# Conv-attention-MoE hybrid: q product in natural order, two softmax shifts on TensorE, the apply by quarters

## The reference

```python
q = einsum('bchw,oc->bohw', x, wq) + bq     # 16 channels
k = einsum('bchw,oc->bohw', x, wk) + bk     # 16 channels
v = einsum('bchw,oc->bohw', x, wv) + bv     # 128 channels
energy = einsum('bci,bcj->bij', qf, kf).reshape(b, h, w, h, w)
attn = softmax(energy, axis=-1)             # over the last 16
out = einsum('bchk,bhwkv->bcwv', v, attn)
x = gamma * out + x
```

## Time and profile before

| | us |
|---|---|
| median of 3 runs | 186.25 (186.21 to 189.31) |
| the profiled execution, its own time | 186.13 |
| its span, first to last instruction | 184.2 |
| outside the span | 1.9 |

### The profile page before, as it was taken

One profiled execution on the slowest core, in us unless ns is written; L12 is line 12 of the kernel. 1 busy time (PEld: TensorE's weight loads), 2 busy tenths in 40 slices (PEclk: granted clock), 3 DMA queues, 4 the chain that ended last, 5 costly groups with the idle time before them and its releaser, 6 DMA issues.

```text
span 184.2 us, 3336 instructions
## 1 busy us (share of the span) xinstructions
PE 174.1 (95%) x1277; PEld 118.6 (64%) x1277; DVE 117.1 (64%) x199; ACT 123.2 (67%) x185; POOL 79.5 (43%) x68
## 2 busy tenths in 40 slices
PE   6999999989898998999999999999999999999991
PEld 3267867665466544447466567567887888888880
DVE  1569544985465396456084959397888677676673
ACT  3516953317727743545988598867878999999970
POOL 8404228988703284452536093524151152333312
PEclk9999999999999999999999999999999999999999
DMA  5799200000000000570000000000000880000001
GB/s 141 276 374 419 96 0 0 4 0 4 0 5 0 2 0 4 181 271 7 0 0 5 0 0 0 4 0 0 0 7 4 244 269 0 0 4 0 0 0 57
DMA packets 5791, 10.94 MB, mean 59 GB/s; under 512 B 1280, under 2 KB 1664, under 8 KB 5520
## 3 DMA queue, kind: packets, MB, share of 16 engines
q1 hardware_dynamic: 5360, 10.65, 16.7%
q10 hardware_dynamic: 416, 0.08, 0.3%
HBM read 10.17 MB, written 0.56 MB: 58 GB/s over the span
## 4 chain that ended last, share of the span: by engine, by line
PE 73%; issue 8%; ACT 7%; POOL 4%; DVE 4%; DMA 2%; ACTq 0%; DVEq 0%; POOLq 0%
PE PS L1159 9%; PE PS L1163 7%; PE PS L1160 7%; PE PS L1186 6%; PE PS L1189 6%; PE PS L1187 6%; PE PS L1181 4%; POOL pairs L357 4%; PE PS L1017 3%; PE PS L1031 3%; ACT room L516 2%; PE PS L910 2%; PE PS L878 2%; PE PS L1104 2%; DMA convw_sb<-convw 2%
## 5 line engine op out<-in xcount | busy, mean ns | idle before, releaser
L516 ACT ACTIVATE room<-PS,b_sb 128x512 f32<-128x512 f32 x64 | 43.6, 688 | 22.6 <-PE PS L1163 21.2
L772 DVE TENSOR_TENSOR Gl<-room,Gh 128x512 fp32r<-128x512 f32 x50 | 41.2, 831 | 13.7 <-ACT Gh L461 13.0
L365 POOL TENSOR_TENSOR x_sb<-x_sb,room 128x512 f32<-128x512 f32 x15 | 23.6, 1572 | 56.0 <-DVE room L781 56.0
L1159 PE MATMUL PS<-x2h,w1h 128*128 128x512 f32 x64 | 27.4, 427 | 1.2 <-ACT room L516 0.8
L461 ACT ACTIVATE Gh<-room 128x512 fp32r<-128x512 f32 x40 | 25.3, 633 | 1.3
L1163 PE MATMUL PS<-x2l,w1h 128*128 128x512 f32 x64 | 25.5, 398 | 0.0
L1160 PE MATMUL PS<-x2h,w1l 128*128 128x512 f32 x64 | 25.2, 393 | 0.0
L1186 PE MATMUL PS<-Gh,w2h 128*128 128x512 f32 x50 | 20.8, 416 | 0.0
L1187 PE MATMUL PS<-Gh,w2l 128*128 128x512 f32 x50 | 19.8, 395 | 0.0
L1189 PE MATMUL PS<-Gl,w2h 128*128 128x512 f32 x50 | 19.7, 395 | 0.0
L1159 PEld LDWEIGHTS PS<-x2h,w1h 128*128 128x128 f32 x64 | 12.0, 187 | 10.6 <-issue 4.9
(11 more groups left out here) (136 smaller groups left out, 294.2 us busy)
## 6 DMA issues: line engine op xcount, KB each, us to landing
room<-comb_rows SPq DMA_DIRECT2D x16, 256.0 KB, 5.2
w1raw<-w SPq DMA_DIRECT2D x8, 256.0 KB, 5.9
w_sb<-w SPq DMA_DIRECT2D x2, 1024.0 KB, 10.6
x_sb<-x SPq DMA_DIRECT2D x2, 256.0 KB, 3.2
dev<-xk SPq DMA_DIRECT2D x1, 512.0 KB, 6.3
out<-x_sb SPq DMA_DIRECT2D x2, 256.0 KB, 4.2
attw_sb<-attw SPq DMA_DIRECT2D x1, 320.0 KB, 6.8
cst<-consts SPq DMA_DIRECT2D x1, 228.5 KB, 6.5
```

The lines of the kernel that those rows point to most:

```text
L365: nc.gpsimd.tensor_tensor(t2[:, cols(p)], t2[:, cols(p)], part[:, s, :], ALU.add).then_inc(acc_done, 1)
L516: nc.scalar.activation(G[:, n % GR, :], PS[:, U_BANK[n % 2], :], ACT.Gelu, bias=b1_sb[:, c:c + 1])\
L772: nc.vector.tensor_tensor(Gl[:, n % GR, :], G[:, n % GR, :], Gh[:, n % GR, :].bitcast(f32), ALU.subtract)\
L1159: mm(o, w1h[e][:, ms], x2h[:, cols(p)], start=True, stop=False)
```

## The change

- q is computed with x in its natural order; the copies by ScalarE and VectorE now read PSUM with h innermost, a stride of 16 elements (`by_columns`), and write `cq` as before.
- `shift(q)` for q = 2 and 3 only takes the negated maximum; TensorE adds it to bank q by a product of the identity with the maxima, each repeated 16 times (`subtract_max`), and ScalarE's exp reads PSUM. VectorE's order becomes shift 0, 1, 2, sums 0, shift 3, sums 1, 2, 3, scale 3.
- The constants' load has a semaphore of its own (`ident_in`).
- `conv_values` goes by halves of two blocks, with its own place in the order; the turns stand between them.
- `conv_apply` goes by quarters: 4 calls of 32 products each, with 64 moving columns in place of 128. All four stand behind the last values.

```diff
-            sp.dma_start(cst[:, :], consts).then_inc(cst_in, 16)
+            sp.dma_start(cst[:, :], consts).then_inc(ident_in, 16)
...
-                nc.scalar.activation(cq[0:C8, pair, :, :, 0].rearrange("c b w h -> c (b w h)"), PS[64:64 + C8, p, :],
+                nc.scalar.activation(cq[0:C8, pair, :, :, 0], by_columns(PS[64:64 + C8, p, :]),
...
             def conv_exp(q):
-                act.wait_ge(shifted, q + 1)
-                nc.scalar.activation(A[:, q * W4:(q + 1) * W4, :, :], S[:, q], ACT.Exp).then_inc(exp_ready, 1)
+                if q < DVE_SHIFTS:
+                    act.wait_ge(shifted, q + 1)
+                    src = S[:, q]
+                else:
+                    act.wait_ge(lowered, q - DVE_SHIFTS + 1)
+                    src = PS[:, q, :].rearrange("p (w k v) -> p w k v", w=W4, k=K8)
+                nc.scalar.activation(A[:, q * W4:(q + 1) * W4, :, :], src, ACT.Exp).then_inc(exp_ready, 1)
...
-                nc.vector.tensor_scalar(cq[32:32 + C8, pair, :, :, 1].rearrange("c b w h -> c (b w h)"),
-                                        PS[64:64 + C8, p, :], convb_sb[64:64 + C8, 0:1], None, ALU.add)\
+                nc.vector.tensor_scalar(cq[32:32 + C8, pair, :, :, 1], by_columns(PS[64:64 + C8, p, :]), convb_sb[64:64 + C8, 0:1], None, ALU.add)\
...
             def shift(q):
-                nc.vector.tensor_reduce(cmax[:, q], e, AX.X, ALU.max).then_inc(cmax_ready, 1)
+                nc.vector.tensor_reduce(cmax[:, q], e, AX.X, ALU.max, negate=(q >= DVE_SHIFTS)).then_inc(cmax_ready, 1)
+                if q >= DVE_SHIFTS:
+                    return
...
-            shift(0)
-            shift(1)
+            for q in range(3):
+                shift(q)
             sums(0)
-            shift(2)
+            shift(3)
             sums(1)
-            shift(3)
             sums(2)
             sums(3)
             scale(3)
...
-                mm(PS[64:64 + C8, p, :].rearrange("c (b w h) -> c b w h", b=2, w=W),
-                   convw_sb[:, 0:C8], x_sb[:, cols(p)].rearrange("c (b h w) -> c b w h", b=2, h=H),
-                   start=True, stop=True)
+                mm(PS[64:64 + C8, p, :], convw_sb[:, 0:C8], x_sb[:, cols(p)], start=True, stop=True)
...
+            def subtract_max(q):
+                pe.wait_ge(ident_in, 16)
+                pe.wait_ge(cmax_ready, q + 1)
+                mm(PS[:, q, :].rearrange("p (g v) -> p g v", v=W), ident,
+                   cmax[:, q].unsqueeze(2).broadcast_to([128, W4 * K8, W]),
+                   start=False, stop=True, skip_group_check=True).then_inc(lowered, 1)
...
-            def conv_apply(g):
-                if g == 0:
+            def conv_apply(q):
+                if q == 0:
                     pe.wait_ge(vT_ready, 2)
-                pe.wait_ge(A_ready, 2 + g)
-                if g:
+                if q < WQ - 1:
+                    pe.wait_ge(A_ready, q + 1)
+                else:
                     pe.wait_ge(last_A_ready, 1)
                 for k in range(K8):
                     for b in range(B):
                         rows = slice(32 * b, 32 * (b + 1))
-                        last = mm(PS[:, 4 + b, g * 128:(g + 1) * 128], vT[rows, k, :],
-                                  A[rows, 8 * g:8 * (g + 1), k, :], start=(k == 0), stop=(k == K8 - 1))
+                        last = mm(PS[:, 4 + b, q * 64:(q + 1) * 64], vT[rows, k, :],
+                                  A[rows, W4 * q:W4 * (q + 1), k, :], start=(k == 0), stop=(k == K8 - 1))
...
-            for q in range(WQ):
-                energy(q)
-                turn(1)
-            for i in range(2):
-                conv_values(i)
-            turn(2)
-            conv_apply(0)
-            turn(1, 0)
-            conv_apply(1)
-            pe.wait_ge(cst_in, 64)
+            energy(0)
+            turn(1)
+            energy(1)
+            conv_values(0, 0)
+            energy(2)
+            energy(3)
+            subtract_max(2)
+            conv_values(0, 1)
+            turn(1)
+            subtract_max(3)
+            conv_values(1, 0)
+            turn(1)
+            conv_values(1, 1)
+            turn(1)
+            for q in range(WQ):
+                conv_apply(q)
+            pe.wait_ge(cst_in, 48)
```

More of the change, by code:

```diff
@@ L151, in hybrid_program @@
         convw_in, attw_in, cst_in = sem("convw_in"), sem("attw_in"), sem("cst_in")
+        ident_in, lowered = sem("ident_in"), sem("lowered")
         w1_in, w2_in = [sem(f"w1_in{e}") for e in range(E)], [sem(f"w2_in{s}") for s in range(2)]
@@ L192, in cols, with by_columns @@
             return slice(p * HALF, (p + 1) * HALF)
+        def by_columns(images):
+            return images.rearrange("c (b h w) -> c b w h", b=2, h=H)
         RAW_BANKS = [((4, 5), (6, 7)), ((2, 3), (4, 5)), ((6, 7), (2, 3)), ((4, 5), (6, 7))]
@@ L219, in hybrid_program @@
         WARM_BANK = [3, 4, 0, 1]
+        DVE_SHIFTS = 2
         U_BANK, Y_BANK, GATE_BANK = (0, 1), (2, 3), (3, 4)
@@ L539, in _ @@
             norm_dev(2)
-            act.wait_ge(cst_in, 64)
+            act.wait_ge(ident_in, 16)
+            act.wait_ge(cst_in, 48)
             for n in range(2):
@@ L622, in _ @@
             scale(3)
-            dve.wait_ge(cst_in, 64)
+            dve.wait_ge(ident_in, 16)
+            dve.wait_ge(cst_in, 48)
             dve.wait_ge(gamma_in, 16)
@@ L879, in energy, with conv_values @@
                                   cq[:, b, W4 * q + w, :, :].rearrange("c h k -> c (h k)"), ck[:, b, :],
-                                  start=True, stop=True)
+                                  start=(w == 0), stop=(q < DVE_SHIFTS and w == W4 - 1), skip_group_check=True)
                 last.then_inc(energy_done, 1)
-            def conv_values(i):
-                if i == 0:
+            def subtract_max(q):
[4 more added lines that the diff above has]
+                   start=False, stop=True, skip_group_check=True).then_inc(lowered, 1)
+            def conv_values(i, half):
+                if i == 0 and half == 0:
                     pe.wait_ge(xk_in_s, 16)
-                for k in range(4 * i, 4 * i + 4):
+                for k in range(4 * i + 2 * half, 4 * i + 2 * half + 2):
                     last = mm(PS[:, 4 + i, (k % 4) * C:(k % 4 + 1) * C], x_k[:, k, :], convw_sb[:, QK:QK + C],
                               start=False, stop=True, skip_group_check=True)
-                    if k % 4 == 1:
-                        turn(1)
-                last.then_inc(vT_done, 1)
+                if half:
+                    last.then_inc(vT_done, 1)
             def conv_bias(i):
@@ L909, in conv_apply @@
                         rows = slice(32 * b, 32 * (b + 1))
-                        last = mm(PS[:, 4 + b, g * 128:(g + 1) * 128], vT[rows, k, :],
-                                  A[rows, 8 * g:8 * (g + 1), k, :], start=(k == 0), stop=(k == K8 - 1))
-                        if g and k == K8 - 1:
+                        last = mm(PS[:, 4 + b, q * 64:(q + 1) * 64], vT[rows, k, :],
+                                  A[rows, W4 * q:W4 * (q + 1), k, :], start=(k == 0), stop=(k == K8 - 1))
+                        if q == WQ - 1 and k == K8 - 1:
                             last.then_inc(conv_done, 1)
```

## The result

The changed kernel takes 189.38 us (median of 5 runs, 189.09 to 190.21) against 186.25: the ratio is 1.0171, interval 1.014 to 1.0201, so it is slower by some 3.1 us. (Runs in a slower state of the chip, such as the 189.31 of before, are left out of all ratios.) The prediction said 188.8, 2.7 slower.

What follows compares the result with a forecast made beforehand. TensorE, busy 95% of the span, was taken as the bound. Apply start 18.25 plus 7.35 plus 0.15 drain gave 25.75 against 23.05, so 186.13 + 2.7 = 188.8 us; range 187.0 to 190.3.

Steps and rivals of the forecast that it cites:

- The mark and the pass-through: End of conv's apply on TensorE, 23.05 before: whatever moves it moves the run; forecast 25.75, +2.7 us, no slack behind.
- Part 4: Apply by quarters: 256 records in place of 128, each still costing its weight load, 28.8 ns; 7.35 us plus 0.15 drain.
- Rival A: Apply: half the columns cost half the time, loads hidden by the stream; -0.75, 185.4 us; chance 0.09.
- Part 1: q projection on TensorE: contiguous records 0.43 against 0.86, ending 1.7 us earlier; waiting for bv cuts the gain to 0.75.
- Part 2: Two subtractions moved from VectorE, 0.61 each there, to TensorE: four records of 0.43, 1.72 us in all.
- rival C: Subtractions on TensorE: the repeated operand streams at half rate, 1.7 us more, 190.5 us; chance 0.05.
- rival B: Copies of q: strided PSUM reads cost double, energy(0) starts at 9.75 after all; +0.75, 189.5 us; chance 0.10.
- From energy(0) to the apply: TensorE's energies, subtractions, turns and values, then ScalarE's copy: energy(0) at 9.0, apply(0) at 18.25, against 18.50 before.
- Part 3: VectorE's saved 1.2 us is lost because exp 3 follows the values' copy on ScalarE; scaling done at about 21.1, before 20.91.
- Rival D: TensorE idles from 6.3 to 7.25, so the clock drops to 1.2 GHz; 4 us lose 2, 190.8 us; chance 0.04.

Runs made afterwards that it cites:

- experiment 1: The changed kernel with only its apply put back to two halves of 128 moving columns: 186.39 us, ratio to before 0.9997.
- experiment 2: The kernel before with only its apply cut into quarters of 64 moving columns: 189.41 us, ratio 1.0189.
- experiment 5: The changed kernel's apply with 32 of 64 moving columns: 192.23 us, repeated 195.66; separately with 64 of 128 weight columns: 187.63 us, repeated 187.76.
- experiment 4: The changed kernel with the two q products repeated behind the apply, contiguous and then with stride 16, results unread: 194.04 us in one run.
- experiment 6: The kernel of experiment 1 with exp 3 moved ahead of the last values' copy on ScalarE: 186.01 us, ratio to before 0.9975.

## Why the prediction was right, and where not

- **The mark and the pass-through**: right. The 3.99 us at the end of conv are the 4.0 of the span. In this execution conv ends at 27.04 where 25.75 was forecast: 1.22 of that stands ahead of energy(0), 0.27 behind it up to the apply, and the apply took 0.20 less.
- **Part 4, the apply**: right, and for the reason given. Forecast 7.35 and 0.15 of drain, measured 7.30. That the load sets the record was argued there from load lengths and from one-column products; experiments 1, 2 and 5 show it. Rival A is out. One step of the argument was misread: "loads of 128 columns 187, with 32 rows as with 128" is not what the earlier trace rows shows, where the loads with 128 rows (L938, L1044) have medians of 136 and 140 ns. Those are the transposes; the loads of L855 with 128 rows last 186 to 192 ns at the full clock in the same trace, so the reading holds for ordinary products and the result did not suffer. Without the drain the measured apply is 7.15, between the 6.85 worked out from the Trainium skill (TensorE: Matmul & The Clock Gate, "LDWEIGHTS (loading the stationary operand)") and my 7.35.
- **Part 1**: the step that failed is "a strided q record occupies 0.86, twice the contiguous one", taken as a gain of 0.43 on each record. The stride's price was right at full rate (experiment 4), but the rows of before could not show it: the projection runs before TensorE has reached that rate, so the contiguous records took 0.85 there for the most part. The price for the contiguous record came from the bias product, which stands later, so the comparison set a record at half rate beside one at full rate. I had taken the full clock from the profile's clock row, which says 1.00 there; the first turns' own loads would have told otherwise. A smaller error stands beside it: from the start of the bias product to energy(0) it takes 1.80 to 1.89 in the profiled executions and not 1.72. Of the forecast gain of 0.75, 0.54 is left in experiment 4 (bv after 5.5 us, energy(0) at 9.21) and 0.27 in experiment 1 (5.8 us, 9.48), and in the profiled execution of the changed kernel a bv later than usual made it a loss of 0.47. The term was mis-sized by 0.2 to 1.2 us, where the whole forecast was 0.6 under the median. That this failure cost so little is no merit of its reasoning: the wait for bv had capped the term at 0.75 of the 1.7, and most of the change is the apply's (2.75 of 3.99).
- **Part 2**: right. The two subtractions take 0.93 and 0.85 (15.29 to 16.22 and 16.91 to 17.76), forecast 0.86 each; rival C is out. The strided copies from PSUM take 708 and 748 ns where they took 734 and 748; rival B is out. The sentence of the Trainium skill (Advanced Engine Details and Errata, "PSUM Cachelines") speaks of matmuls, and for copies by ScalarE and VectorE these rows show no such price.
- **From energy(0) to the apply**: 9.52, forecast 9.25. Nearly every step is within 0.05 of its price; 0.08 was lost ahead of the first subtraction, 0.08 in it, and 0.15 from the last values to the start of their copy.
- **Part 3**: right. Exp 3 waited behind the values' copy, and VectorE idled 1.63 us; experiment 6 moved it and won 0.4.
- **Rival D**, a fall of the clock in the wait for bv: not seen in the changed kernel, where TensorE was idle for 0.24 us there and not for the 0.95 forecast, nor in experiment 6, where it was idle for 0.59. No run shows the 4 us that it took for such a stretch. The clock fell where I had not looked for it, with 32 moving columns and TensorE busy, which is not the mechanism of D.

## What to carry to other kernels

Before a product is cut along its moving columns, compare the stream with the load of its weights: with 128 weight columns in a 32-row strip these f32 records cost 28 to 29 ns at 128, 64 and 32 moving columns, and only fewer weight columns made them cheaper. A price read late in a kernel does not hold in its first microseconds; compare like records at the place itself. And time saved on one engine has to be followed through the order of the engine that it feeds before it is counted.

## What the runs showed of the hardware

- TensorE starts at half rate although the clock row says 1.00. The loads of the first turns (L868) beside those of later turns, and beside the loads of the warm products (L1004) that ran while the clock was granted at 0.50, all from the repeat with 32 moving columns; durations in ns, min/median/max, then first and last start in us:

```profile
L868 PEld LDWEIGHTS PS<-x2h x5: 288/329/338, 1.5 to 2.9; 128*128 128x128 f32 x5
L868 PEld LDWEIGHTS PS<-x2h x5: 186/192/192, 7.8 to 18.5; 128*128 128x128 f32 x5
L1004 PEld LDWEIGHTS PS<-w1h x2: 287/310/333, 31.5 to 31.6; 128*128 128x128 f32 x2
```

The early loads last as long as those at 0.50, the 1.2 GHz level, and not the 186 to 192 of the 2.4 GHz level. It is not the DMA traffic that slows them: in the changed kernel the DMA engines are as busy from 8 to 20 us (shares of 1.05 and 1.00) as before it (0.88 from 2 to 4 us), and the bias product's contiguous records are 0.43 apart there.
- With 32 moving columns under 128-column weights, TensorE busy without a gap, the granted clock fell to 0.50 in both executions, some 5 and 2 us into the apply; with 64 columns it stayed at 1.00 through the apply in the profiled ones. At 0.50 the record cost 54 ns.
- At 14.9 ns a record TensorE stopped for 1.3 and 1.4 us after 174 of 256 records in both executions. The cause is open.
- The landing of one small DMA (bv, 64 KB) took 5.3 to 6.6 us in different executions. TensorE waits for it only where the projection is done first: by 0.24 us in the changed kernel's profiled execution (6.6), by 0.59 in that of experiment 6 (5.8).
